# Value sums of two key blocks in one run on TensorE, every eighth step, in three attention layers

## The chip, the cores and the metric

The kernel runs on one core of one Trainium2 chip. The metric is device time in microseconds of one execution; lower is better. One core has TensorE (PE in the profile; its weight loads are PEld), VectorE (DVE), ScalarE (ACT), GpSimd (POOL) and SyncE (SP, which issues the DMAs here). Each has its own queue and runs it in order; the engines meet only at semaphores.

## The reference

Eight batches of 512 tokens, 256 wide, go through eight layers, each added to its input. Three of them are multi-head attention with 16 heads of 16, and only these are touched:

```python
x = x + _L0_attn_a_ref(_layernorm(x), ...)   # "decay": scores scaled by exp(-0.01*|t-s|)
x = x + _L0_ffn_ref(...)
x = x + _L0_attn_b_ref(_layernorm(x), ...)   # "rope"
x = x + _L0_ffn_ref(...)
x = x + _L1_attn_a_ref(...)                  # "causal", one head
x = x + _L1_ffn_ref(...)
x = x + _L1_attn_b_ref(_layernorm(x), ...)   # "latent": rotary, factored k and v
x = x + _L1_ffn_ref(...)

# inside each of the three, for b batches and 16 heads
scores = jnp.einsum('bhqd,bhkd->bhqk', q, k) * scale
attn = jax.nn.softmax(scores, axis=-1)
out = jnp.einsum('bhqk,bhkd->bhqd', attn, v)
out = out.transpose(0, 2, 1, 3).reshape(b, s, d) @ Wo
```

## The kernel before

`mha_layer` builds each of the three layers. A batch has four groups of four heads, and each group has four blocks of 128 keys. This makes 16 blocks of a batch, counted `kk` = 0 to 15, and 64 steps `s` = 0 to 63, one for each block and head. All engines run the same list of steps; what an engine does at a step is written out by hand in its own `body`.

At a step TensorE does, in this order:

- `exp_scores` (L1331, in decay L1334 and L1337): the transposed scores, keys by queries, of one head and key block, into one of two banks of `psB` ("scores_k"). It waits until ScalarE has taken the scores of two steps earlier.
- at some steps `value_sums` (L1362): four products, one for each head, of 32 columns of `Vaug` (values and ones) with the probabilities of one block, into four strips of one bank `psO` ("out_heads"). In fp32 each product is two instructions, so one call is a run of 8 matmuls.
- `max_scores` (L1318): the scores of a later group, queries by keys, for its row maxima, into a ring of banks of `psA` ("scores_q"): three banks in rope and latent, two in decay. It waits until VectorE has taken the maximum of the bank's last user.
- at the steps in `USES` one piece of `work`: projections for the next batch (L1281, L1286), transposes (L1277, L1292, L1297, L1300) and the output projection (L1305).

ScalarE takes each `exp_scores` into `probs` (L1489, "probs") and copies the work out. It starts a block only when `value_sums` of the block whose place in `probs` it takes is done; `probs` has `PSLOTS` places, three in decay and two in the others. VectorE takes a row maximum at each step (L1570, in decay L1567), splits the maxima of a group at one step in 16 (L1590 to L1597), normalises heads (L1604, L1606), adds the output (L1619 to L1627) and rotates keys and queries (L1553 to L1556); the rest of the rotation is on GpSimd.

In decay the diagonal of a block needs other scores: after every fourth `exp_scores` TensorE makes four products of 128 columns (L1347) into a bank of its own, ScalarE exponentiates them, and VectorE merges them into `probs` (`merge_diagonal`, L1579). The next four products (L1347) wait for that merge, since they write the same bank.

`value_sums` of block `kk` stands at step 4(`kk`+1) + `PV_AT`, and `PV_AT` is 2 in rope and latent, 3 in decay: at steps 2, 6, 10, ... 62, or 3, 7, 11, ... 63, where the one at step 2 or 3 belongs to the last block of the batch before. Four of them in a row make a group, after which ScalarE copies `psO` to `Osb` (L1480) and the heads' transposes may start.

Of the kernel before, what the change touches and what calls it, by code (L numbers as in the profile page):

```python
# [13 lines left out]
NB, S, D = 8, 512, 256  # L14
# [953 lines left out]
def mha_layer(nc, g, ins, decay, scale, project_q, biased, aside=(), results=None):  # L968
# [25 lines left out]
    if decay:  # L994
        PV_AT = 3
# [4 lines left out]
    elif project_q:  # L1000
        PV_AT = 2
# [4 lines left out]
    else:  # L1006
        PV_AT = 2
# [11 lines left out]
    A_BANK = [a % A_RING for a in range(63)] + [1]  # L1019
    A_LAST = [max(i for i in range(-64, a) if A_BANK[i % 64] == A_BANK[a]) for a in range(64)]  # L1020
    ROW_DMAS = NV
    PSLOTS = 3 if decay else 2
    XN = 4 if project_q else 8
    KQ = ["k0", "q0", "k1", "q1"] if project_q else ["k0", "k1"]
    PRO = ["xT0", "xT1"] + KQ + ["v0", "v1"]
    PREV = ["OT3", "aT0", "aT1", "Wo0", "Wo1"]
    assert USES == sorted(USES) and {n for _, n in USES} == {*PRO, *PREV, "OT0", "OT1", "OT2", "mT0", "mT1", "mT2", "mT3"}
    MID = [n for _, n in USES]
    ORDER = {"pre": PRO + ["mT0"], "first": [n for n in MID if n not in PREV], "mid": MID,
             "last": [n for n in MID if n not in PRO + ["mT0"]], "post": PREV}  # L1030
# [20 lines left out]
    def bank(tag, b, name):  # L1051

        return use(tag, 1 if tag == "mid" else b, name) % 2

    def emptied(tag, b, name):

        if tag != "mid":
            return use(tag, b, name) // 2 + 1
        return (b - 1) * (len(MID) // 2) + (use(tag, 1, name) // 2 + 1)

    def groups(s, tag, at):


        return [(g // 4, g % 4, a) for g in range(6) for a in range(len(at[g % 4])) if 16 * g + at[g % 4][a] == s
                and not (tag == "last" and g > 3)]

    with ExitStack() as ctx:
        def sb(name, shape, dt):
            return ctx.enter_context(nc.sbuf_tensor(f"{g['layer']}_{name}", shape, dt))
# [16 lines left out]
        KS = sb("KS", [99, NV, 2, 8, S], BF16)  # L1086
        probs = sb("probs", [P, PSLOTS, 4, S], F32)
        Vaug = sb("Vaug", [P, 2, 4, H, 32], F32)
# [171 lines left out]
        def _(pe):  # L1260
# [48 lines left out]
            def max_scores(nb, grp, a):  # L1309

                k = grp * NAG + a
                if a == 0:
                    pe.wait_ge(grp_loaded[grp], (nb + 1) * (16 * 2 * NV))
                if not (isinstance(nb, int) and nb * 64 + A_LAST[k] < 0):
                    pe.wait_ge(a_done, nb * 64 + (A_LAST[k] + 1))
                c, (qt, h) = grp // 2, divmod(a, 4)
                hh = 4 * (grp % 2) + h
                pe.matmul(psA[:, A_BANK[k], :], QS[0:96, 0, c, hh, qt * P:(qt + 1) * P],  # L1318
                          KS[0:96, NV - 1, c, hh, :], start=True, stop=True).then_inc(a_ready, 1)
# [31 lines left out]
            def value_sums(b, kk):  # L1351

                grp, kt = kk // 4, kk % 4
                if kk == 0:
                    for of in ("v0", "v1"):
                        at = ("pre", 0, of) if b == 0 else ("first" if b == 1 else "mid", b - 1, of)
                        pe.wait_ge(m_taken[bank(*at)], emptied(*at))
                if kt == 0 and not (isinstance(b, int) and b * 4 + grp < 1):
                    pe.wait_ge(o_taken, b * 4 + grp)
                pe.wait_ge(merged if decay else exp_done, (b * 16 + (kk + 1)) * (1 if decay else 4))  # L1360
                for h in range(4):
                    last = pe.matmul(psO[32 * h:32 * h + 32, :], Vaug[:, b % 2, kt, 4 * grp + h, :],  # L1362
                                     probs[:, (b * 16 + kk) % PSLOTS, h, :], start=(kt == 0), stop=(kt == 3))
                last.then_inc(pv_done, 1)
# [17 lines left out]
            def body(tag, b):  # L1382
                for s in range(64):
                    grp, o = divmod(s, 16)
                    exp_scores(b, s)
                    if o % 4 == PV_AT:
                        if s > PV_AT:
                            value_sums(b, s // 4 - 1)
                        elif tag != "first":
                            value_sums(b - 1, 15)  # L1390
                    for ahead, of, a in groups(s, tag, A_AT):
                        max_scores(b + ahead, of, a)
                    for at, name in USES:
                        if at == s and name in ORDER[tag]:
                            nb = b - 1 if name in PREV else b + 1 if name in PRO + ["mT0"] else b
                            work(tag, b, nb, name)

            body("first", 0)
            for b in range(1, NB - 1):
                body("mid", b)  # L1400
            body("last", NB - 1)
            value_sums(NB - 1, 15)
            for name in ORDER["post"]:
                work("post", NB, NB - 1, name)

# [2 lines left out]
        def _(act):  # L1408
# [73 lines left out]
            def body(tag, b):  # L1482
                for s in range(64):
                    grp, o = divmod(s, 16)
                    kk, h = s // 4, s % 4
                    if h == 0 and not (isinstance(b, int) and b * 16 + kk < PSLOTS):
                        act.wait_ge(pv_done, b * 16 + kk - PSLOTS + 1)
                    act.wait_ge(b_ready, b * 64 + (s + 1))
                    act.activation(probs[:, (b * 16 + kk) % PSLOTS, h, :], psB[:, s % 2, :], ACT.Exp, scale=scale).then_inc(  # L1489
                        exp_done, 1)  # L1490
# [27 lines left out]
        def _(dve):  # L1518
# [53 lines left out]
            def merge_diagonal(b, kk):  # L1572

                kt = kk % 4
                if b * 16 + kk == 0:
                    dve.wait_ge(later_set, 2)
                dve.wait_ge(exp_done, b * 64 + (4 * kk + 4))
                dve.wait_ge(e_exp, b * 16 + (kk + 1))
                dve.copy_predicated(probs[:, (b * 16 + kk) % PSLOTS, :, kt * P:(kt + 1) * P],  # L1579
                                    later[:, :].bitcast(mybir.dt.uint32).unsqueeze(1).to_broadcast([P, 4, P]),  # L1580
# [478 lines left out]
def hybrid_stack(nc, w, out):  # L2059

    with ExitStack() as ctx:
# [19 lines left out]
        with layer("decay"):  # L2081
            mha_layer(nc, g, decay, True, 1.0 / D ** 0.5, True, False, clears(g, w["zeros"]))
# [4 lines left out]
        with layer("experts1"):  # L2087
            routed_layer(nc, g, experts_a, False, then=lambda results: named(
                "rope", mha_layer, rope, False, HD ** -0.5, True, False, (), results))
        with layer("experts2"):  # L2090
            routed_layer(nc, g, experts_a, False, then=lambda results: named("causal", single_head_layer, causal, results))
        with layer("experts3"):
            routed_layer(nc, g, experts_b, True, then=lambda results: named(
                "latent", mha_layer, latent, False, HD ** -0.5, False, True, (), results))
# [75 lines left out]
```

## Time and profile before

| | |
|---|---|
| median of 3 runs | 3416.64 us (3415.6 to 3421.77) |
| the profiled execution | 3420.55 us, of which the span is 3418.5 us |
| PE busy | 2686.4 us (79%) |
| DVE busy | 1931.8 us (57%) |
| ACT busy | 1487.5 us (44%) |
| POOL busy | 780.6 us (23%) |
| out_heads matmuls | 1024 in each of decay, rope and latent, 137 to 148 us busy each |
| decay, first to last out_heads | 115.9 to 804.3 us |
| rope | 1091.4 to 1638.8 us |
| latent | 2486.0 to 3031.0 us |

The busy time of a matmul in these records is longer than the time it keeps the next one away, since matmuls are pipelined: the distance from one start to the next tells what a matmul costs TensorE. So a busy share near 100% does not mean that TensorE never waits. A row of a timeline gives the start, the duration, the engine, the line, what is written and read, how many alike were merged, and in brackets the idle time before it with what ended it.

### The profile page before, as it was taken

Reading aid. Unit: us, or ns where it says so; the run is one execution under the profiler, and the core shown is the slowest. Engines: PE = TensorE matmul, PEld = TensorE weight load, DVE = VectorE, ACT = ScalarE, POOL = GpSimd, SP = SyncE. Lnnn points to the kernel's source line nnn. Section 1 sums busy time; section 2 is a strip of 40 time slices with the busy share of each in tenths; the row PEclk is TensorE's granted clock in tenths of the full one; section 3 lists DMA queues with packets and bytes.
Section 4 is the critical chain, followed back from the end, with each engine's and each line's share of the span. In section 5 each row is a group of like instructions: output and inputs, shape, how many; then the busy total and the mean of one; then the engine's idle time right before and its main releaser. Section 6 shows DMA issues by size and latency. Waiting matters only on the chain. (4 is left out here: it accounts for less than half of the span.)

```text
span 3418.5 us, 40272 instructions
## 1 busy us (share of the span) xinstructions
PE 2686.4 (79%) x12980; PEld 1387.0 (41%) x12980; DVE 1931.8 (57%) x4955; ACT 1487.5 (44%) x2908; POOL 780.6 (23%) x742
## 2 busy tenths in 40 slices
PE   4868888896566999999555784898398999974993
PEld 2324443444342333333344564565133333343662
DVE  4757777785338778787342442111778788741112
ACT  2446666665223666666522431111166566640110
POOL 0312222210313322240123003000334323203003
PEclk6779999999687999999787895899599999986997
DMA  7555554441244322222134002232422332202333
GB/s 236 172 175 149 149 150 148 142 132 42 87 140 123 109 87 85 84 84 66 56 109 134 1 1 85 97 111 71 119 75 86 113 91 83 77 9 98 111 111 111
DMA packets 213575, 351.27 MB, mean 103 GB/s; under 512 B 21192, under 2 KB 168265, under 8 KB 208632
## 3 DMA queue, kind: packets, MB, share of 16 engines
q1 hardware_dynamic: 197864, 299.02, 28.0%
q0 software_dynamic: 15504, 49.68, 4.4%
q8 instruction: 107, 1.75, 0.2%
q14 instruction: 100, 0.82, 0.1%
HBM read 203.21 MB, written 154.80 MB: 105 GB/s over the span
## 5 line engine op out<-in xcount | busy, mean ns | idle before, releaser
L1567 DVE CUSTOM_DVE_ANT_0 decay_junk<-decay_scores_q,decay_corr 128x512 bf16<-128x512 f32 x512 | 338.9, 685 | 159.0 <-PE decay_scores_q L1318 157.5
L1489 ACT ACTIVATE decay_probs<-decay_scores_k 128x512 f32<-128x512 f32 x512 | 298.7, 602 | 229.3 <-PE decay_scores_k L1337 179.2
L1570 DVE TENSOR_REDUCE rope_mx<-rope_scores_q 128x1 f32<-128x512 f32 x512 | 326.5, 684 | 106.6 <-PE rope_scores_q L1318 106.6
L1489 ACT ACTIVATE latent_probs<-latent_scores_k 128x512 f32<-128x512 f32 x512 | 292.6, 600 | 207.4 <-PE latent_scores_k L1331 206.6
L1489 ACT ACTIVATE rope_probs<-rope_scores_k 128x512 f32<-128x512 f32 x512 | 293.0, 600 | 204.3 <-PE rope_scores_k L1331 203.5
L1570 DVE TENSOR_REDUCE latent_mx<-latent_scores_q 128x1 f32<-128x512 f32 x512 | 326.9, 684 | 96.8 <-PE latent_scores_q L1318 96.8
L1318 PE MATMUL latent_scores_q<-latent_KS,latent_QS 96*128 96x512 bf16 x512 | 204.1, 401 | 73.9 <-DVE latent_mx L1570 59.3
L1318 PE MATMUL decay_scores_q<-decay_KS,decay_QS 96*128 96x512 bf16 x512 | 213.8, 418 | 48.6 <-DVE decay_mx L1567 32.5
L1318 PE MATMUL rope_scores_q<-rope_KS,rope_QS 96*128 96x512 bf16 x512 | 202.7, 398 | 42.9 <-DVE rope_mx L1570 33.8
L1331 PE MATMUL latent_scores_k<-latent_QS,latent_KS 99*128 99x512 bf16 x512 | 197.0, 387 | 10.4 <-ACT latent_probs L1489 6.3
L1331 PE MATMUL rope_scores_k<-rope_QS,rope_KS 99*128 99x512 bf16 x512 | 196.5, 386 | 9.0 <-ACT rope_probs L1489 6.3
L1334 PE MATMUL decay_scores_k<-decay_QS,decay_KS 99*128 99x384 bf16 (+3 forms) x512 | 160.5, 315 | 54.1 <-ACT decay_probs L1489 26.9
L1318 PEld LDWEIGHTS latent_scores_q<-latent_KS,latent_QS 96*128 96x128 bf16 x512 | 50.1, 98 | 248.4 <-DVE latent_mx L1570 180.1
L1362 PE MATMUL decay_out_heads<-decay_probs,decay_Vaug 128*32 128x512 f32 x1024 | 147.8, 652 | 0.8 <-DVE decay_probs L1579 0.8
L1318 PEld LDWEIGHTS decay_scores_q<-decay_KS,decay_QS 96*128 96x128 bf16 x512 | 51.4, 101 | 228.4 <-DVE decay_mx L1567 164.1
L1362 PE MATMUL latent_out_heads<-latent_probs,latent_Vaug 128*32 128x512 f32 x1024 | 139.7, 618 | 0.7 <-ACT latent_probs L1489 0.7
L1362 PE MATMUL rope_out_heads<-rope_probs,rope_Vaug 128*32 128x512 f32 x1024 | 137.1, 608 | 0.7 <-ACT rope_probs L1489 0.7
L1318 PEld LDWEIGHTS rope_scores_q<-rope_KS,rope_QS 96*128 96x128 bf16 x512 | 50.2, 98 | 207.4 <-DVE rope_mx L1570 144.3
L1166 POOL CAST decay_parts<-decay_fc 128x512 bf16<-128x512 f32 x56 | 34.2, 611 | 410.9 <-DVE decay_fc L1553 398.9
L495 POOL DMA_INDIRECT experts_XN<-cap_results,experts_back x64 | 63.0, 984 | 262.5 <-DMA cap_results<-experts4x_y 243.5
L344 POOL DMA_INDIRECT cap_dispatched<-experts_XN,experts_slot x64 | 62.9, 983 | 250.3 <-SPq L58 200.2
L624 PE MATMUL experts4x_inner<-experts4x_xT,experts4x_w 128*128 128x512 f32 x256 | 113.4, 602 | 0.8 <-ACT experts4x_xT L662 0.8
(450 smaller groups left out, 5318.5 us busy)
## 6 DMA issues: line engine op xcount, KB each, us to landing
decay_parts_dram<-decay_parts SPq DMA_DIRECT2D x64, 384.0 KB, 2.6
decay_KS<-decay_parts_dram SPq DMA_DIRECT2D x64, 384.0 KB, 6.1
decay_QS<-decay_parts_dram SPq DMA_DIRECT2D x64, 384.0 KB, 6.6
decay_parts_dram<-decay_parts SPq DMA_DIRECT2D x64, 256.0 KB, 2.9
experts3x_w<-in_w_dram SPq DMA_DIRECT2D x16, 1024.0 KB
experts4x_w<-in_w_dram SPq DMA_DIRECT2D x16, 1024.0 KB
rope_parts_dram<-rope_parts SPq DMA_DIRECT2D x32, 384.0 KB, 2.9
rope_KS<-rope_parts_dram SPq DMA_DIRECT2D x32, 384.0 KB, 4.0
```

The lines of the kernel that those rows point to most:

```text
L344: pool.indirect_dma_start(out=xe, out_offset=bass.IndirectOffsetOnAxis(ap=g["slot"][:, i:i + 1], axis=0), in_=g["XN"][:, i, :], in_offset= ...
L495: pool.indirect_dma_start(out=g["XN"][:, i, :], out_offset=None, in_=ye, in_offset=bass.IndirectOffsetOnAxis(ap=g["back"][:, i:i + 1], axi ...
L624: last = pe.matmul(psH[:, f % 2, :], w1[:, p, c, f * P:(f + 1) * P], xT[:, p, c, :], start=(c == 0), stop=(c == 1))
L1166: eng.tensor_copy(parts[:, (nb * NCH + j) % RING, 0, :], fc[:, j % 2, :]).then_inc(p0_done, 1)
L1318: pe.matmul(psA[:, A_BANK[k], :], QS[0:96, 0, c, hh, qt * P:(qt + 1) * P], KS[0:96, NV - 1, c, hh, :], start=True, stop=True).then_inc(a_r ...
L1331: last = pe.matmul(psB[:, s % 2, :], KS[:, 0, c, hh, keys], QS[:, 0, c, hh, :], start=True, stop=True)
L1334: last = pe.matmul(psB[:, s % 2, 0:end], KS[:, 1, c, hh, keys], QS[:, 0, c, hh, 0:end], start=True, stop=True)
L1362: last = pe.matmul(psO[32 * h:32 * h + 32, :], Vaug[:, b % 2, kt, 4 * grp + h, :], probs[:, (b * 16 + kk) % PSLOTS, h, :], start=(kt == 0) ...
L1489: act.activation(probs[:, (b * 16 + kk) % PSLOTS, h, :], psB[:, s % 2, :], ACT.Exp, scale=scale).then_inc(exp_done, 1)
L1567: dve.tensor_tensor_reduce(junk[:, a % 2, :], psA[:, A_BANK[k], :], corr[:, qt, :], 1.0, -3.0e38, ALU.mult, ALU.max, mx[:, grp % 2, qt, h: ...
L1570: dve.tensor_reduce(mx[:, grp % 2, qt, h:h + 1], psA[:, A_BANK[k], :], AX.X, ALU.max).then_inc(a_done, 1)
```

## The change

In all three layers `probs` gets three places (`PSLOTS`), and the value sums of two blocks are made one after the other, at every eighth step: blocks 2m and 2m+1 at step 8(m+1) + `PV_AT`. In rope and latent the runs at steps 6, 14, 22, ... 62 go, and those at 2, 10, 18, ... 58 are twice as long; in decay those at 7, 15, ... 63 go, and those at 3, 11, ... 59 are twice as long. What is computed, every other instruction and every other place stay.

```diff
-    PSLOTS = 3 if decay else 2
+    PSLOTS, PV_BLOCKS = 3, 2
...
-                    if o % 4 == PV_AT:
-                        if s > PV_AT:
-                            value_sums(b, s // 4 - 1)
-                        elif tag != "first":
-                            value_sums(b - 1, 15)
+                    if s % (4 * PV_BLOCKS) == PV_AT:
+                        for kk in range(s // 4 - PV_BLOCKS, s // 4):
+                            if s > PV_AT:
+                                value_sums(b, kk)
+                            elif tag != "first":
+                                value_sums(b - 1, 16 + kk)
...
             body("last", NB - 1)
-            value_sums(NB - 1, 15)
+            for kk in range(16 - PV_BLOCKS, 16):
+                value_sums(NB - 1, kk)
```

TensorE in the rope layer, a batch in the middle, from step 38 to step 42, before ("x4" counts the products of one call; L1331 is `exp_scores`, L1318 `max_scores`):

```order
L1331 MATMUL rope_scores_k<-rope_QS,rope_KS 128x512
L1362 MATMUL rope_out_heads<-rope_probs,rope_Vaug 32x512 x4
L1318 MATMUL rope_scores_q<-rope_KS,rope_QS 128x512
L1331 MATMUL rope_scores_k<-rope_QS,rope_KS 128x512
L1318 MATMUL rope_scores_q<-rope_KS,rope_QS 128x512
L1331 MATMUL rope_scores_k<-rope_QS,rope_KS 128x512
L1318 MATMUL rope_scores_q<-rope_KS,rope_QS 128x512
L1292 MATMUL rope_work<-identb,rope_mp 12x128 x4
L1331 MATMUL rope_scores_k<-rope_QS,rope_KS 128x512
L1318 MATMUL rope_scores_q<-rope_KS,rope_QS 128x512
L1331 MATMUL rope_scores_k<-rope_QS,rope_KS 128x512
L1362 MATMUL rope_out_heads<-rope_probs,rope_Vaug 32x512 x4
```

And after, the same steps:

```order
L1331 MATMUL rope_scores_k<-rope_QS,rope_KS 128x512
L1318 MATMUL rope_scores_q<-rope_KS,rope_QS 128x512
L1331 MATMUL rope_scores_k<-rope_QS,rope_KS 128x512
L1318 MATMUL rope_scores_q<-rope_KS,rope_QS 128x512
L1331 MATMUL rope_scores_k<-rope_QS,rope_KS 128x512
L1318 MATMUL rope_scores_q<-rope_KS,rope_QS 128x512
L1292 MATMUL rope_work<-identb,rope_mp 12x128 x4
L1331 MATMUL rope_scores_k<-rope_QS,rope_KS 128x512
L1318 MATMUL rope_scores_q<-rope_KS,rope_QS 128x512
L1331 MATMUL rope_scores_k<-rope_QS,rope_KS 128x512
L1362 MATMUL rope_out_heads<-rope_probs,rope_Vaug 32x512 x8
```

The run at step 38 has moved behind everything up to step 42 and stands there with the run that was there already.

TensorE in the decay layer, from the run at step 43 to `max_scores` of step 47, before (L1347 is the products of the diagonal):

```order
L1362 MATMUL decay_out_heads<-decay_probs,decay_Vaug 32x512 x4
L1318 MATMUL decay_scores_q<-decay_KS,decay_QS 128x512
L1334 MATMUL decay_scores_k<-decay_QS,decay_KS 128x512
L1318 MATMUL decay_scores_q<-decay_KS,decay_QS 128x512
L1334 MATMUL decay_scores_k<-decay_QS,decay_KS 128x512
L1318 MATMUL decay_scores_q<-decay_KS,decay_QS 128x512
L1334 MATMUL decay_scores_k<-decay_QS,decay_KS 128x512
L1318 MATMUL decay_scores_q<-decay_KS,decay_QS 128x512
L1334 MATMUL decay_scores_k<-decay_QS,decay_KS 128x512
L1347 MATMUL decay_scores_q<-decay_QS,decay_KS 128x128 x4
L1362 MATMUL decay_out_heads<-decay_probs,decay_Vaug 32x512 x4
L1318 MATMUL decay_scores_q<-decay_KS,decay_QS 128x512
```

And after:

```order
L1362 MATMUL decay_out_heads<-decay_probs,decay_Vaug 32x512 x8
L1318 MATMUL decay_scores_q<-decay_KS,decay_QS 128x512
L1334 MATMUL decay_scores_k<-decay_QS,decay_KS 128x512
L1318 MATMUL decay_scores_q<-decay_KS,decay_QS 128x512
L1334 MATMUL decay_scores_k<-decay_QS,decay_KS 128x512
L1318 MATMUL decay_scores_q<-decay_KS,decay_QS 128x512
L1334 MATMUL decay_scores_k<-decay_QS,decay_KS 128x512
L1318 MATMUL decay_scores_q<-decay_KS,decay_QS 128x512
L1334 MATMUL decay_scores_k<-decay_QS,decay_KS 128x512
L1347 MATMUL decay_scores_q<-decay_QS,decay_KS 128x128 x4
L1318 MATMUL decay_scores_q<-decay_KS,decay_QS 128x512
```

The run at step 43 is twice as long, and none stands between the diagonal and `max_scores` of step 47.

## Rows read from the trace of the kernel before

**Rows 1.** The profile page: its first line.

```profile
span 3418.5 us, 40272 instructions
```

**Rows 2.** Stretch and length; busy PE, PEld, DVE, ACT, POOL; clock; DMA share, GB/s.

```profile
230.00:760.00 530.00, 471.66 (x2862) 213.62 (x2858) 411.42 (x1178) 345.24 (x653) 139.75 (x144) 0.95 0.49 145
1120.00:1610.00 490.00, 462.14 (x2431) 176.70 (x2430) 389.15 (x788) 317.85 (x597) 135.98 (x121) 1.00 0.29 88
```

**Rows 3.** Who waited for whom: total us, times, longest; TensorE.

```profile
PE rope_scores_q L1318 <- DVE rope_mx L1570: 33.8, 29, 7.8
PE decay_scores_q L1347 <- DVE decay_probs L1579: 19.4, 22, 2.1
```

**Rows 4.** The costliest groups of the page: one layer's value sums.

```profile
L1362 PE MATMUL rope_out_heads<-rope_probs,rope_Vaug 128*32 128x512 f32 x1024 | 137.1, 608 | 0.7 <-ACT rope_probs L1489 0.7
```

**Rows 5.** Timeline of rope, step 6 of a middle batch: TensorE and its weight loads.

```profile
1303.62 0.38 PE L1331 MATMUL rope_scores_k<-rope_QS,rope_KS 99*128 99x512 bf16 x1
1303.93 1.07 PE L1362 MATMUL rope_out_heads<-rope_probs,rope_Vaug 128*32 128x512 f32 x8
1304.92 0.39 PE L1318 MATMUL rope_scores_q<-rope_KS,rope_QS 96*128 96x512 bf16 x1
...
1303.92 0.16 PEld L1362 LDWEIGHTS rope_out_heads<-rope_probs,rope_Vaug 128*32 128x32 f32 x8 [0.64 <-issue]
```

**Rows 6.** Timeline of rope, steps 42 to 46: TensorE, then ScalarE.

```profile
1349.91 0.39 PE L1318 MATMUL rope_scores_q<-rope_KS,rope_QS 96*128 96x512 bf16 x1
1350.13 0.38 PE L1331 MATMUL rope_scores_k<-rope_QS,rope_KS 99*128 99x512 bf16 x1
...
1352.02 1.06 PE L1362 MATMUL rope_out_heads<-rope_probs,rope_Vaug 128*32 128x512 f32 x8
1353.02 0.39 PE L1318 MATMUL rope_scores_q<-rope_KS,rope_QS 96*128 96x512 bf16 x1
...
1350.55 2.17 ACT L1489 ACTIVATE rope_probs<-rope_scores_k 128x512 f32<-128x512 f32 x4 [0.43 <-PE rope_scores_k L1331]
```

**Rows 7.** Timeline of rope, steps 38 to 42: TensorE, then VectorE.

```profile
1347.52 0.39 PE L1318 MATMUL rope_scores_q<-rope_KS,rope_QS 96*128 96x512 bf16 x1 [0.70 <-DVE rope_mx L1570]
...
1346.78 1.28 DVE L1570 TENSOR_REDUCE rope_mx<-rope_scores_q 128x1 f32<-128x512 f32 x2
```

**Rows 8.** Timeline of decay, steps 45 to 48: VectorE, then TensorE.

```profile
459.62 0.72 DVE L1579 COPY_PREDICATED decay_probs<-decay_later,decay_scores_q 128x512 f32<-128x512 uint32 x1
460.24 0.67 DVE L1567 CUSTOM_DVE_ANT_0 decay_junk<-decay_scores_q,decay_corr 128x512 bf16<-128x512 f32 x1
...
462.16 0.69 DVE L1567 CUSTOM_DVE_ANT_0 decay_junk<-decay_scores_q,decay_corr 128x512 bf16<-128x512 f32 x1 [0.62 <-PE decay_scores_q L1318]
...
457.97 0.39 PE L1318 MATMUL decay_scores_q<-decay_KS,decay_QS 96*128 96x512 bf16 x1
...
460.40 0.40 PE L1347 MATMUL decay_scores_q<-decay_QS,decay_KS 99*128 99x128 bf16 x4
460.73 1.07 PE L1362 MATMUL decay_out_heads<-decay_probs,decay_Vaug 128*32 128x512 f32 x8
461.73 0.39 PE L1318 MATMUL decay_scores_q<-decay_KS,decay_QS 96*128 96x512 bf16 x1
```

**Rows 9.** Timeline of decay, steps 15 to 19, TensorE; then a stretch's clock.

```profile
414.18 1.06 PE L1362 MATMUL decay_out_heads<-decay_probs,decay_Vaug 128*32 128x512 f32 x8
...
418.66 0.29 PE L1334 MATMUL decay_scores_k<-decay_QS,decay_KS 99*128 99x128 bf16 x1 [2.65 <-ACT decay_probs L1489]
...
421.97 1.94 PE L1362 MATMUL decay_out_heads<-decay_probs,decay_Vaug 128*32 128x512 f32 x8
...
417.80:421.20 3.40, 2.08 (x8) 0.80 (x9) 1.31 (x3) 3.40 (x8) 2.90 (x4) 0.50 0.28 94
```

**Rows 10.** Timeline of rope, step 24, TensorE; then a stretch of latent, step 26.

```profile
1326.86 0.39 PE L1318 MATMUL rope_scores_q<-rope_KS,rope_QS 96*128 96x512 bf16 x1 [1.54 <-DVE rope_mx L1570]
...
2718.40:2721.80 3.40, 3.40 (x13) 0.81 (x12) 2.07 (x4) 2.06 (x4) 2.61 (x3) 0.50 0.31 103
```

## The prediction

> **What bounds the kernel now.** I read the busy shares by stretch, then the waits, then timelines of a batch in the middle. The profiled execution took 3420.55 us, 3418.5 of them span [rows 1] and 2 around it; the median of the runs, 3416.64, is 3.91 us lower, and I add what the trace gives to the median as it is. In the steady part of rope TensorE is busy 462 of 490 us, VectorE 389 and ScalarE 318; in decay 472, 411 and 345 of 530 [rows 2]. TensorE leads, but the busy time of pipelined matmuls flatters it, and the waits show that it isn't alone: in rope it stands 33.8 us behind VectorE's maxima, in decay 19.4 us behind the merge of the diagonal alone [rows 3]. So for each stretch of a batch one has to ask which engine ends last in it. A step below is one of a batch's 64.
>
> **What joining saves.** A layer has 1024 out_heads matmuls in runs of 8 [rows 4], so 128 runs; 64 of them move to stand behind another, 192 in the three layers. A score matmul keeps the next one away for 0.22 us (1349.91 to 1350.13 [rows 6]), but the run for 0.31: 1303.62 to 1303.93. So the way in costs 0.09. The next matmul starts at 1304.92, 0.99 later; I use 1.00 [rows 5]. One of the eight takes 0.61 [rows 4] and the whole run 1.07 [rows 5], so the second wave of four starts 0.45 after the first. Two waves are 0.90, and 0.10 is the way out. Both ends are late weight loads: the run's starts at 1303.92, with its matmul and not ahead of it [rows 5]. A run of 16 is then 1.00 + 2 x 0.45 = 1.90, and a pair costs 0.09 + 1.90 = 1.99 in place of 2 x 1.09 = 2.18: **0.19 us less**. No row shows a run of 16 without a wait inside. The bounds are 0 (the second call pays both ends again) and 0.19 (nothing but the ends can go); I take 0.19, as the strips stay the same. In all 192 x 0.19 = 36 us: the ceiling.
>
> The Trainium skill, "TensorE: Matmul & The Clock Gate", section "Step-by-step: what each phase is for", says that a weight load is pulled ahead of running matmuls if its rows don't conflict or it goes to the background buffer. If that held here, the ends would not be late loads and joining would save nothing. The late load of [rows 5] speaks against it where the shape of the tiles changes.
>
> **What the third place saves.** Nothing that I can find: the wait of ScalarE in [rows 6] is for scores, not for out_heads. With the joined run a block still finds its place free: block 2m+3 starts after the run that holds block 2m. So it adds no wait either. SyncE's, GpSimd's and VectorE's instructions keep their order; no DMA is moved past another.
>
> **What bunching costs.** TensorE now gives no scores for 0.31 + 1.90 = 2.2 us and then runs eight steps without a pause. ScalarE has two banks of scores ahead of it, VectorE three (two in decay). They run dry in the long run and hold TensorE up between runs. Where TensorE is the bound, a removed run is 1.09 less and a doubled one 0.90 more. Where it isn't, the first may give nothing.
>
> *Rope and latent, steps 43 to 50: ScalarE.* Four steps take 1353.02 - 1349.91 = 3.11 us; four exponentials take 2.17 and one about 0.60, so they follow each other at (2.17 - 0.60) / 3 = 0.52 [rows 6]. With no run between, four more steps go at 0.52 each, 2.09, where TensorE alone would need 4 x 0.44 = 1.76. A pair: 3.11 + 2.09 + 0.90 = 6.10, in place of 6.22: **0.1 less**.
>
> *The same, steps 36 to 42: VectorE.* Step 40's `max_scores` waits 0.70 for VectorE, which works without a gap up to the two maxima at 1346.78 [rows 7]. The run of step 38 lies under that work. Taken away it frees nothing, as the same maximum releases step 40; the doubled run at 42 stands in the open. **0.9 more.**
>
> *Steps 14 to 26.* VectorE's long stretch begins with `max_scores` of step 14, which comes 1.09 sooner. The runs at 18 and 22 lie under it: step 24 waits 1.54 [rows 10]. The run of 26 is open, 0.90 longer: 0.2 less. Step 10: 0.2 less in rope, and 0.3 in latent, where VectorE is still busy and lets only part of the 1.09 through. Steps 34, 58 and 2: about 0. A batch: rope -0.1 + 0.9 - 0.2 - 0.2 = **+0.4**, latent **+0.3**.
>
> *Decay, steps 43 to 59: the merge.* VectorE merges at 459.62 and is done at 460.24; the diagonal goes at 460.40, the run at 460.73, the next `max_scores` at 461.73, and VectorE takes it up at 462.16 after 0.62 idle. Four steps are 461.73 - 457.97 = 3.76, and outside the 0.62 VectorE never rests [rows 8]: 1.24 in two loops. After: from merge to maximum 1.92 + 0.90 = 2.82, of which two waiting maxima cover 1.92 - 0.62 = 1.30, so 1.52 idle, and none at the other diagonal. **0.3 more** a pair; at 51 nothing covers it.
>
> *Decay, steps 11 to 27.* At step 16 TensorE stands 2.65 us behind ScalarE [rows 9]. By the code ScalarE waits there for VectorE's fourth rotation, which stands behind the maximum of step 15, which stands behind the run at 414.18; that run goes, so 1.09 sooner. But right behind this idle time the granted clock is 0.50, the 1.2 GHz level, and step 19's run lies there: 1.94 us in place of 1.07 [rows 9]. Doubled it is 1.8 more. From there VectorE bounds it to step 26, so the removal at 23 gives nothing, and the doubling at 27 costs 0.90. Sum -1.1 + 1.8 + 0.9 = **+1.6**. Bounds: -0.4 (two pairs that keep their 0.19) and +2.7 (nothing comes sooner at 16).
>
> *The rest of decay.* Step 3: +0.2, 11: -0.2, 35: +0.1, 59: 0, by the same working. Step 43: -0.3, between -0.9 and +0.9, since the removed run of 39 lies partly open at the low clock. A batch of decay: 0.3 + 1.6 - 0.2 = **+1.7**.
>
> **The sum.** I count seven batches of a layer like the middle ones: 7 x (1.7 + 0.4 + 0.3) = 16.8. The last batch has hardly any maxima, so four steps are about 3.11 - 0.22 = 2.89; a pair goes from 5.78 to 2.89 + 2.09 + 0.90 = 5.88, 0.1 x 8 pairs x 3 layers = 2.4. Together 19 us: **3436 us**. I prefer this to the ceiling because behind most removed runs that I followed another engine's wait comes within a few steps.
>
> **Rivals.** *Faster: TensorE is the bound after all.* The place is the removed runs of steps 22, 38 and their like. If the banks were deep enough that VectorE gets through sooner when scores come sooner, each pair would keep its 0.19: 36 us, 3380; with half the pairs 18 us, 3399. It decides as soon as the waits behind removed runs grow by less than 0.9 us. For it: a busy share of 94% in rope [rows 2]. Against: [rows 3] and [rows 7].
>
> *No change: the costs are half of mine.* With -0.4 in place of +1.6 in decay the sum is 19 - 14 = 5 us, and with half the price at step 42 (14 batches x 0.45 = 6) it is 0: 3410 to 3423. For it: that term has the widest bounds.
>
> *Slower still: the clock.* TensorE's wait at step 24 in rope grows from 1.54 us to some 2.6, as the run of 22 goes and the maximum comes no sooner relative to it [rows 10]. Decay's clock was down behind 2.65 us of standing [rows 9], latent's is in step 26 already, rope's isn't. A stretch of 3.40 us fully busy at 0.50 [rows 10] loses 1.7: in seven batches of rope 12 us, as much again in latent if it comes twice: 3447 to 3460. The skill's section "Loop structure matters more than you think" on that page warns of waits between matmuls in the same sense; the 0.50 of [rows 9] agrees.
>
> **How the numbers follow.** Forecast (3424 to 3447) 0.44; TensorE bound 0.20; no change 0.22; clock 0.14. The range 3396 to 3460 leaves out the better half of the first rival and the tail of the last. 0.2% of 3416.64, 6.8 us, is about what a measurement can tell from no change; it holds the no-change case. Faster 0.20, same 0.22, slower 0.58.
>
> **What would show it.** A run of 16: 1.90 from its start to the next matmul, and 0.31 ahead of it. Rope: the wait of step 40 near 1.8, that of step 24 over 2; steps 43 to 50 in 6.1 us, decay's in 7.8. Decay: step 19's run lasts near 3.7. I am wrong if TensorE's waits behind L1567 and L1570 don't grow, or if rope's batches get shorter.

## The result and the profile after

The median of the changed kernel is 3479.91 us (5 runs, 3478.73 to 3485.95) beside 3415.6 us (5 runs, 3414.2 to 3421.77) of the kernel before: 64 us more, a ratio of 1.0191 with a 95% interval of 1.0177 to 1.0205. The direction was forecast; the size was not: 19 us more were forecast, and the range ended at 3460. Lines of the kernel from L1403 on stand two lines later than before.

The page's first lines, beside [rows 1]:

```profile
span 3484.0 us, 40270 instructions
...
PE 2733.9 (78%) x12980; PEld 1420.7 (41%) x12980; DVE 1926.4 (55%) x4955; ACT 1483.4 (43%) x2908; POOL 784.6 (23%) x742
```

The stretch of decay of [rows 2] and one of rope like the one there, 3 us longer, then the three layers from the start of their first exponential to that of their last (stretch and length; busy PE, PEld, DVE, ACT, POOL; granted clock; DMA share, GB/s):

```profile
230.00:760.00 530.00, 466.36 (x2735) 216.12 (x2735) 389.27 (x1131) 329.57 (x624) 139.68 (x143) 0.92 0.48 143
1132.00:1625.00 493.00, 458.75 (x2327) 181.83 (x2325) 373.52 (x753) 301.19 (x568) 139.41 (x125) 0.95 0.30 89
...
104.40:821.30 716.90, 611.51 (x3592) 280.81 (x3590) 500.81 (x1449) 435.72 (x825) 169.81 (x172) 0.91 0.46 140
1100.40:1676.90 576.50, 533.39 (x2700) 209.17 (x2698) 427.73 (x865) 355.76 (x670) 157.75 (x140) 0.96 0.26 78
2515.30:3090.70 575.40, 518.91 (x2644) 192.29 (x2642) 434.14 (x889) 350.39 (x656) 173.78 (x146) 0.96 0.26 78
```

The three layers before:

```profile
105.00:801.20 696.20, 596.77 (x3592) 267.71 (x3590) 508.52 (x1449) 437.26 (x825) 168.12 (x172) 0.92 0.47 144
1083.00:1638.70 555.70, 519.35 (x2707) 197.28 (x2709) 425.95 (x862) 358.23 (x671) 157.28 (x140) 0.99 0.27 81
2478.00:3029.70 551.70, 505.58 (x2652) 188.05 (x2650) 432.88 (x888) 351.88 (x657) 171.39 (x146) 0.98 0.27 81
```

They grew by 20.7, 20.8 and 23.7, together 65.2 of the 65.5 us by which the span grew. So all of it lies in the layers that were changed, and 42 us of it in TensorE's busy time (1621.7 to 1663.8), though nothing was added for it to do. The clock of rope's steady part is 0.95 where it was 1.00 [rows 2].

TensorE's waits, beside [rows 3]:

```profile
PE latent_scores_q L1318 <- DVE latent_mx L1572: 61.7, 44, 23.4
PE rope_scores_q L1318 <- DVE rope_mx L1572: 37.7, 27, 7.9
PE decay_scores_q L1318 <- DVE decay_mx L1569: 36.5, 81, 10.6
...
PE decay_scores_q L1347 <- DVE decay_probs L1581: 19.0, 24, 2.1
```

The maxima are waited for 2 to 4 us longer in each layer (33.8 us before in rope, 59.3 in latent, 32.5 in decay), the merge as long as before (19.4). Waits alone don't hold 65 us. The timelines show the rest. Rope, steps 24 to 26 of a middle batch, TensorE; the second fence has the clock of the stretches around it:

```profile
1348.48 0.39 PE L1331 MATMUL rope_scores_k<-rope_QS,rope_KS 99*128 99x512 bf16 x1
1351.29 0.61 PE L1318 MATMUL rope_scores_q<-rope_KS,rope_QS 96*128 96x512 bf16 x1 [2.42 <-DVE rope_mx L1572]
...
1353.74 3.64 PE L1362 MATMUL rope_out_heads<-rope_probs,rope_Vaug 128*32 128x512 f32 x16
1357.31 0.61 PE L1318 MATMUL rope_scores_q<-rope_KS,rope_QS 96*128 96x512 bf16 x1
```

```profile
1347.60:1351.00 3.40, 1.24 (x5) 0.29 (x3) 3.30 (x6) 1.85 (x4) 3.26 (x4) 1.00 0.00 0
1351.30:1354.70 3.40, 3.40 (x16) 0.98 (x20) 2.91 (x6) 1.71 (x4) 2.21 (x3) 0.50 0.09 32
1354.70:1358.10 3.40, 3.40 (x18) 0.94 (x11) 0.14 (x1) 0.35 (x1) 1.10 (x1) 0.51 0.61 203
```

TensorE is busy 1.24 of 3.40 us while it waits for VectorE, and behind that the granted clock is 0.50, the 1.2 GHz level, for almost 7 us. The doubled run lies there: 3.57 us from 1353.74 to 1357.31. The trace of before has the same place at full clock in five of its six middle batches, with a run of 1.00 us.

The same batch, steps 38 to 43, where the clock was full:

```profile
1374.57 0.39 PE L1318 MATMUL rope_scores_q<-rope_KS,rope_QS 96*128 96x512 bf16 x1 [0.93 <-DVE rope_mx L1572]
...
1375.89 0.39 PE L1318 MATMUL rope_scores_q<-rope_KS,rope_QS 96*128 96x512 bf16 x1 [0.70 <-DVE rope_mx L1572]
...
1376.97 0.38 PE L1331 MATMUL rope_scores_k<-rope_QS,rope_KS 99*128 99x512 bf16 x1
1377.28 1.92 PE L1362 MATMUL rope_out_heads<-rope_probs,rope_Vaug 128*32 128x512 f32 x16
1379.14 0.39 PE L1318 MATMUL rope_scores_q<-rope_KS,rope_QS 96*128 96x512 bf16 x1
```

This gives the price of a run of 16: 0.31 ahead of it and 1.86 to the next matmul; at the 1.2 GHz level it is 3.58. It also shows where the removed run went: a wait of 0.93 at step 39, with the 0.70 of step 40 as in [rows 7].

Decay, step 16, the run of step 19, the wait of step 24's maximum, and the run of step 27:

```profile
424.58 0.23 PE L1334 MATMUL decay_scores_k<-decay_QS,decay_KS 99*128 99x128 bf16 x1 [2.65 <-ACT decay_probs L1491]
...
427.81 2.80 PE L1362 MATMUL decay_out_heads<-decay_probs,decay_Vaug 128*32 128x512 f32 x16
430.54 0.39 PE L1318 MATMUL decay_scores_q<-decay_KS,decay_QS 96*128 96x512 bf16 x1
...
435.77 0.39 PE L1318 MATMUL decay_scores_q<-decay_KS,decay_QS 96*128 96x512 bf16 x1 [0.90 <-DVE decay_mx L1569]
...
441.24 1.92 PE L1362 MATMUL decay_out_heads<-decay_probs,decay_Vaug 128*32 128x512 f32 x16
```

The 2.65 us of [rows 9] are unchanged. The doubled run took 2.73 us here, two thirds of that time at the low clock, and 3.3 to 3.6 in the five other middle batches.

### The profile page after: what moved, and what is told of

The parts are those of the page before. It is cut to its first block and busy times, and to the rows that moved or that the text cites. A ratio compares the mean times of both kernels' runs of the same rounds, so it can differ in the third digit from the quotient of the medians.

```text
span 3484.0 us, 40270 instructions
## 1 busy us (share of the span) xinstructions
PE 2733.9 (78%) x12980; PEld 1420.7 (41%) x12980; DVE 1926.4 (55%) x4955; ACT 1483.4 (43%) x2908; POOL 784.6 (23%) x742
## 5 line engine op out<-in xcount | busy, mean ns | idle before, releaser
L1318 PE MATMUL latent_scores_q<-latent_KS,latent_QS 96*128 96x512 bf16 x512 | 203.5, 399 | 78.6 <-DVE latent_mx L1572 61.7
L1318 PE MATMUL decay_scores_q<-decay_KS,decay_QS 96*128 96x512 bf16 x512 | 212.7, 416 | 52.2 <-DVE decay_mx L1569 36.5
L1318 PE MATMUL rope_scores_q<-rope_KS,rope_QS 96*128 96x512 bf16 x512 | 205.6, 403 | 46.9 <-DVE rope_mx L1572 37.7
L1331 PE MATMUL latent_scores_k<-latent_QS,latent_KS 99*128 99x512 bf16 x512 | 200.2, 392 | 16.8 <-ACT latent_probs L1491 12.3
L1331 PE MATMUL rope_scores_k<-rope_QS,rope_KS 99*128 99x512 bf16 x512 | 200.0, 392 | 12.2 <-ACT rope_probs L1491 7.7
L1334 PE MATMUL decay_scores_k<-decay_QS,decay_KS 99*128 99x384 bf16 (+3 forms) x512 | 161.4, 316 | 55.5 <-ACT decay_probs L1491 30.3
L1318 PEld LDWEIGHTS latent_scores_q<-latent_KS,latent_QS 96*128 96x128 bf16 x512 | 50.2, 98 | 201.1 <-DVE latent_mx L1572 115.9
L1318 PEld LDWEIGHTS decay_scores_q<-decay_KS,decay_QS 96*128 96x128 bf16 x512 | 50.9, 100 | 191.5 <-DVE decay_mx L1569 112.1
L1318 PEld LDWEIGHTS rope_scores_q<-rope_KS,rope_QS 96*128 96x128 bf16 x512 | 50.5, 99 | 163.1 <-DVE rope_mx L1572 91.8
```

Source lines behind the costliest of these rows:

```text
L1331: last = pe.matmul(psB[:, s % 2, :], KS[:, 0, c, hh, keys], QS[:, 0, c, hh, :], start=True, stop=True)
L1334: last = pe.matmul(psB[:, s % 2, 0:end], KS[:, 1, c, hh, keys], QS[:, 0, c, hh, 0:end], start=True, stop=True)
```

## The experiments

All ran on two other chips (e1 to e4 on one, e5 to e10 on the other), where the kernel before took 3333 us. The attention layers are as long there as here (696, 556 and 553 us with only the places changed), so the layers of all traces may be compared; ratios are against the kernel before on the same chip. A ratio rests on 4 to 10 executions of a kernel, its trace on one of them. Most traces are within about 6 us of their kernel's median, but that of e2 is 9 us below the median, the fastest of ten, and that of e6 15 us above it, the slowest of nine. Two edits were used. JOINED names the pairs whose two runs are joined (the pair 8 moves the run of step 6 to step 10 in rope and latent, and that of 7 to 11 in decay; 16, 24 and 40 likewise); all eight are the change itself. FILL repeats a step's `exp_scores` matmul (in decay the product of L1334) so many times in batches 1 to 6, called the middle batches here, with the same operands and the same bank, so that TensorE works where it waited. Shortened:

```diff
+    FILL = {'decay': {16: 38, ...}, 'rope': {24: 10, ...}, 'latent': {...}}[...]
+    JOINED = {'decay': [...], 'rope': [...], 'latent': [...]}[...]
...
+                for i in range(FILL.get(s, 0) if fill else 0):
+                    last = pe.matmul(psB[:, s % 2, :], KS[:, 0, c, hh, keys], QS[:, 0, c, hh, :], start=True, stop=True) \
+                        if not decay else ...
```

What the traces give, in us. "Low" is the time at the 1.2 GHz level in the three layers, from each one's second batch on.

| kernel | ratio, 95% interval | decay | rope | latent | sum | low |
|---|---|---|---|---|---|---|
| before (first chip) | | 696.2 | 555.7 | 551.7 | 1803.6 | 72 |
| after (first chip) | 1.0191 [1.0177, 1.0205] | 716.9 | 576.5 | 575.4 | 1868.8 | 171 |
| e1_places | 1.0005 [0.9987, 1.0023] | 695.7 | 555.5 | 552.8 | 1803.9 | 79 |
| e2_after_fill | 1.0021 [1.0007, 1.0035] | 685.6 | 559.6 | 554.2 | 1799.3 | 10 |
| e3_before_fill | 0.9977 [0.996, 0.9995] | 689.2 | 554.8 | 545.7 | 1789.7 | 17 |
| e4_single42 | 1.0127 [1.0098, 1.0157] | 715.9 | 565.6 | 560.7 | 1842.2 | 140 |
| e5_cross | 1.0115 [1.0085, 1.0144] | 714.5 | 563.5 | 564.0 | 1842.0 | 109 |
| e6_two | 0.995 [0.9933, 0.9966] | 705.9 | 552.1 | 540.3 | 1798.4 | 123 |
| e7_two_fill | 0.989 [0.9862, 0.9918] | 675.5 | 550.8 | 541.5 | 1767.8 | 20 |
| e8_other_two | 1.0192 [1.0161, 1.0224] | 707.0 | 578.1 | 573.9 | 1859.0 | 136 |
| e9_rope24 | 0.9874 [0.9852, 0.9896] | 671.9 | 544.9 | 541.7 | 1758.5 | 3 |
| e10_24filled | 1.0044 [1.0022, 1.0066] | 697.1 | 561.0 | 551.7 | 1809.8 | 24 |

And by place, mean of batches 1 to 5, us from the first exponential of a stretch of steps to the first behind it:

| steps | before | after | e3 | e2 | e9 | e10 |
|---|---|---|---|---|---|---|
| decay 5-12 | 11.78 | 11.40 | 11.78 | 11.40 | 11.40 | 11.78 |
| decay 13-28 | 25.89 | 28.00 | 26.22 | 25.20 | 23.71 | 27.43 |
| decay 37-44 | 11.10 | 12.29 | 10.08 | 10.23 | 10.08 | 10.08 |
| decay 45-60 | 16.69 | 16.98 | 16.71 | 17.00 | 16.71 | 16.70 |
| rope 5-20 | 19.54 | 19.16 | 19.54 | 19.16 | 19.16 | 19.54 |
| rope 21-28 | 12.54 | 14.79 | 12.22 | 12.35 | 11.58 | 13.16 |
| rope 37-44 | 7.41 | 8.93 | 7.41 | 8.27 | 7.41 | 7.41 |
| rope 45-60 | 13.12 | 13.20 | 13.12 | 13.20 | 13.12 | 13.13 |
| latent 5-20 | 18.23 | 18.22 | 18.24 | 18.22 | 18.23 | 18.24 |
| latent 21-28 | 12.68 | 13.59 | 11.72 | 12.02 | 11.18 | 12.57 |
| latent 37-44 | 7.41 | 9.92 | 7.41 | 8.27 | 7.42 | 7.42 |
| latent 53-68 | 16.45 | 16.72 | 16.50 | 16.72 | 16.51 | 16.51 |

**Places alone.**

```diff
-    PSLOTS = 3 if decay else 2
+    PSLOTS = 3
```

> The kernel before with three places for probabilities in all layers and every value sum where it was. Both theories: no difference, ratio within 0.1% of 1, since no wait for a place was seen. If the third place alone costs (another address, another wait), it shows here: then part of the 64 us is not the order of TensorE.

The ratio is 1.0005, with 1 inside its interval, and the layers' sum 0.3 us off: no cost and no gain of the third place can be seen, and everything else below is the joined runs and the filling.

**The change with its idle time filled** (decay 16, 24 and 39; rope 24, 39 and 40; latent 11, 24, 39 and 40).

> The changed kernel, but in batches 1 to 6 some score matmuls are issued again, with the same operands to the same bank, before their semaphore: in decay 38 more at step 16, 4 at 24 and 15 at 39, in rope 10 at 24, 4 at 39, 3 at 40, in latent 5 at 11, 9 at 24, 4 at 39, 3 at 40. They are as long as TensorE stands idle there in the trace after, a little less, and add nothing to the result. Theory clock (the three layers spend 171 us at half clock in the trace after, 72 in that before, and a stretch busy with matmuls loses half of it): half-clock stretches of the three layers fall from 171 us to under 70 and the time by 35 to 60 us, near 3435, where my sum without the clock rival had it. Theory banks alone (only waits and doubled runs that stand open cost, the clock nothing): no gain, 0 to 10 us slower through the added matmuls.

In the traces 69.5 us are gone, more than the change's 65 (1868.8 to 1799.3); by the ratios (1.0191 to 1.0021) it is 57. The only difference is more work for TensorE in its waits. Rope, step 24 to 26, TensorE (L1342 is the repeated matmul, L1320 `max_scores`, L1368 the value sums):

```profile
1279.22 2.32 PE L1342 MATMUL rope_scores_k<-rope_QS,rope_KS 99*128 99x512 bf16 x10
1281.80 0.39 PE L1320 MATMUL rope_scores_q<-rope_KS,rope_QS 96*128 96x512 bf16 x1 [0.26 <-DVE rope_mx L1580]
...
1283.19 1.92 PE L1368 MATMUL rope_out_heads<-rope_probs,rope_Vaug 128*32 128x512 f32 x16
1285.05 0.39 PE L1320 MATMUL rope_scores_q<-rope_KS,rope_QS 96*128 96x512 bf16 x1
```

The maximum of step 24 is waited for until the same point of the batch, but the run behind it takes 1.86 in place of 3.57.

**The kernel before, filled likewise** (decay 16 and 39, rope 24, latent 11 and 24; three places).

> The kernel before with three places and with matmuls issued again in the same way: in decay 38 at step 16 and 15 at 39, in rope 6 at 24, in latent 6 at 11 and 6 at 24, batches 1 to 6. Theory clock: before has 72 us at half clock in the three layers, 48 of them in those batches of decay behind steps 16 and 39; most go, 15 to 30 us faster than before. Theory banks alone: same or up to 5 us slower.

The kernel before gives back 14 us in its layers and 8 by the ratio, less than the 15 to 30 I expected. Set against e2, 55 of the 65 us are the clock by the traces and 10 (1799.3 - 1789.7) the moved runs; by the ratios 49 and 15. Most of the loss is the clock either way; its share is known no closer than that.

In decay the comparison is blurred, for something else came in with the filling: steps 13 to 20 became 1.4 us shorter (14.17 to 12.76), but steps 21 to 28 1.7 longer (11.72 to 13.46). There, in batch 1 of e3 and at full clock, VectorE splits the maxima (two of its four instructions), then GpSimd, then TensorE's wait for the merge that stands behind the split:

```profile
247.25 1.00 DVE L1595 TENSOR_SCALAR decay_mp<-decay_mx 128x16 bf16<-128x16 f32 x1
248.29 1.18 DVE L1597 SCALAR_TENSOR_TENSOR decay_mr<-decay_mx,decay_mp 128x16 f32<-128x16 f32 x1
...
247.06 1.16 POOL L1169 TENSOR_TENSOR decay_rr<-decay_fc,decay_parts 128x512 f32<-128x512 f32 x1
248.28 1.15 POOL L1174 TENSOR_TENSOR decay_parts<-decay_rr,decay_parts 128x512 bf16<-128x512 f32 x1
...
250.57 0.40 PE L1352 MATMUL decay_scores_q<-decay_QS,decay_KS 99*128 99x128 bf16 x4 [2.14 <-DVE decay_probs L1584]
```

In the kernel before each of the four takes 0.17 here. Now two take 1.00 and 1.18, and each ends 0.03 to 0.04 us after the GpSimd instruction beside it. This came in four of e3's six middle batches, and all ten such instructions of its decay layer that took over 0.3 us ran beside one of GpSimd's. Below I call this the slow split. The earlier arrival put them there and lost what it had won; that GpSimd is what holds them is my reading, which no run tests. Rope and latent have two such slow instructions a batch at this place in every kernel (1.25 and 1.13 in rope), so they don't disturb the comparison there.

**One pair single again** (rope and latent without pair 40; all else as the change).

> The changed kernel, but in rope and latent the runs at steps 38 and 42 stay single, as before; all else joined. Theory banks with clock: the open doubled run at 42 goes, 0.86 us in each of 14 batches, 12 us, and with it the half-clock stretches at steps 41 and 42 (2 in rope, 6 in latent, 1.6 us each), 13 us: together 20 to 28 us faster than the changed kernel, and batches of rope near 73.9, of latent near 72.5. Theory clock alone: 13. Theory that every joined pair costs alike (64 us over 192 pairs): 16 pairs make 5 us.

Rope and latent lose 10.9 and 14.7 us of what they had gained in length, 25.6 in 14 batches. e2 and e3 put the open run at 8.27 - 7.41 = 0.86 a batch at full clock, 12 us; the rest is mostly the clock at that place, 0.66 a batch in rope and 1.65 in latent (after against e2). Rope also lost 0.7 a batch in steps 21 to 28 (14.79 to 14.10), which weren't edited.

**The filling crossed** (rope only at 24; latent only at 39 and 40; decay not).

> The changed kernel with matmuls issued again at one place a layer only: in rope 10 at step 24, in latent 4 at 39 and 3 at 40, in decay none; batches 1 to 6. Theory that a half-clock stretch belongs to the idle time just ahead of it: in rope the stretches at steps 24 to 26 go (34 us of half clock in the changed kernel) and those at 41 and 42 stay or become more, in latent those at 42 go (20 us) and those at 24 to 26 stay; decay as in the changed kernel, 717 us long. Rope 560 to 568 us long in place of 577, latent 565 to 568 in place of 576: 17 to 25 us faster than the changed kernel. Theory that it is the mean load of the batch that counts: both places change alike in both layers.

Latent of this kernel, steps 24 to 26, then steps 40 to 42, TensorE:

```profile
2673.11 0.59 PE L1320 MATMUL latent_scores_q<-latent_KS,latent_QS 96*128 96x512 bf16 x1 [2.15 <-DVE latent_mx L1580]
...
2675.55 2.40 PE L1368 MATMUL latent_out_heads<-latent_probs,latent_Vaug 128*32 128x512 f32 x16
...
2677.89 0.39 PE L1320 MATMUL latent_scores_q<-latent_KS,latent_QS 96*128 96x512 bf16 x1
```

```profile
2697.51 1.92 PE L1368 MATMUL latent_out_heads<-latent_probs,latent_Vaug 128*32 128x512 f32 x16
2699.36 0.39 PE L1320 MATMUL latent_scores_q<-latent_KS,latent_QS 96*128 96x512 bf16 x1
```

Where the idle time stood, the run behind it is slow in five of six middle batches (2.34 us here, up to 3.58); where it was filled, 1.86 in every batch. In rope it is the other way round: the run of step 26 takes 1.86 in all middle batches and that of 42 still takes 3.2 to 3.4 in two. Rope is 563.5 and latent 564.0 us long, close to what the first theory had (560 to 568 and 565 to 568). The low clock belongs to the idle time right ahead of it, and not to how hard TensorE works in the layer.

**Only the pairs 8 and 16.**

> Only two pairs of a batch are joined, those whose run goes from steps 6 and 14 to steps 10 and 18 (decay 7 and 15 to 11 and 19); all others single, three places. My theory: a run gains where it is moved from ahead of VectorE's long stretch to under it. Per batch rope -0.24 and -1.1, latent -0.3 and -0.3 to -1.0, decay -0.4 and -1.1 (less 0.8 to 0.9 back where step 19's run is at half clock): rope 547 us long in place of 556, latent 546 to 549 in place of 552, decay 687 to 694 in place of 696. Together 12 to 25 us faster than the kernel before, ratio 0.993 to 0.996. Rival, joining always costs in proportion (64 us over 192 pairs): 48 pairs, 16 us slower. Rival, every join saves its 0.24: 12 us faster, the same in each layer, 4 us.

Faster than the kernel before: 0.995, as expected. The layers of the trace differ from what I expected: latent is shorter (540.3), rope longer (552.1, with 17 us at the low clock behind step 24), and decay 10 us longer than before, with 65 us at the low clock in steps 32 to 47 where the kernel before has 17. Decay, step 39, TensorE:

```profile
449.64 0.61 PE L1348 MATMUL decay_scores_q<-decay_QS,decay_KS 99*128 99x128 bf16 x4 [2.07 <-DVE decay_probs L1584]
450.18 1.94 PE L1363 MATMUL decay_out_heads<-decay_probs,decay_Vaug 128*32 128x512 f32 x8
452.05 0.61 PE L1319 MATMUL decay_scores_q<-decay_KS,decay_QS 96*128 96x512 bf16 x1
```

Nothing is edited there. The kernel before waits the same 2.1 us, and in two of its six middle batches the clock stays full around it; here it is down in all six. But this trace is of the slowest of nine executions. Its mean clock over the whole kernel is 0.886, the median of the nine 0.895, and 0.009 of 3320 us is 60 us more at the low level than in a typical execution (twice the missing share). So decay's low clock here may be that of one bad execution, and it isn't shown that joining elsewhere brings the clock down at this place. What the trace does show is that a wait of about 2 us may or may not bring the clock down. By what that is decided is open.

**The same, filled** (decay 16 and 39, latent 11 and 24).

> The kernel of e6_two and matmuls issued again in batches 1 to 6: in decay 44 at step 16 and 15 at 39, in latent 5 at 11 and 2 at 24. Clock theory: decay loses most of its half-clock stretches (55 us before) and 10 us more against e6_two, near 680; latent 2 to 5 us. Together 25 to 35 us faster than the kernel before, ratio 0.990 to 0.993. Without a part for the clock: as e6_two.

0.989, a little better than expected. Against e3, where decay and latent are filled at the same places and no run is joined, the layers are 22 us shorter (in e7 rope's step 24 isn't filled, which takes some of it back). Not all of that is the two pairs' own: 14 of the 22 are in decay, where e3 has the slow split and 17 us of low clock and e7 has 7.

**Only the pairs 24 and 40.**

> Only the pairs are joined whose run goes from steps 22 and 38 to steps 26 and 42 (decay 23 and 39 to 27 and 43): as many as in e6_two, 48 in all. My theory: both go from under VectorE's stretch into the open, 0.86 each, 1.7 us a batch and layer, 36 us, and 10 to 25 us for the clock, which falls as steps 24 and 39 idle longer: 35 to 60 us slower than the kernel before, ratio 1.011 to 1.018. Rival, cost in proportion: 16 us slower, as e6_two. Rival, each join saves: 12 us faster.

1.0192 (1.0161 to 1.0224): two of the eight pairs make as much as all eight. I expected 1.011 to 1.018.

**e7 and rope filled at 24**, the last place that had a low clock.

> Runs joined only at the pairs of steps 8 and 16, as in the kernel with two joined pairs and filled idle time; added are six repeats of the score matmul in the idle time of step 24 in rope, whose output is written again with the same numbers. Theory (what is left of the half clock in rope, 14 us of it behind step 24, comes from that idle time): rope goes from 550.8 us to 545 to 549, its half clock to under 3 us, the ratio from 0.989 to 0.987 to 0.9885. Rival (the fill only fills, and the half clock there is chance, or the repeats get in the way of the maximum of step 24): rope stays at 550 or more, the ratio at 0.989 or above.

Rope went from 550.8 to 544.9 and its low time to 0; 3 us are left, in decay. This is the fastest kernel here, 0.9874, 1.3% below the kernel before.

**Only the pair 24, filled.**

> Only the pair of step 24 is joined in all three layers (the runs of 22 or 23 go, those of 26 or 27 are doubled), three places, and the idle times of steps 11, 16, 24 and 39 are filled with repeats of the score matmul that write the same numbers. It shows what is left of the cost of the doubled run at step 26 and 27 when the clock stays up. Theory (the run stands in the open there for at most 0.9 us a pair, and the rest of what the kernel with two other pairs lost in steps 21 to 28, 1.7 us a batch in rope and 2.0 in latent, was the clock): steps 21 to 28 take 12.1 to 12.5 us in rope, under 12.3 in latent and 12.5 to 12.7 in decay, the half clock is under 20 us in the three layers, and the ratio is 0.998 to 1.001. Rival (the doubled run itself costs most of it, by holding up ScalarE and VectorE): rope stays above 13 us, latent above 14 in these steps, ratio above 1.005.

```profile
1306.60 1.92 PE L1368 MATMUL rope_out_heads<-rope_probs,rope_Vaug 128*32 128x512 f32 x16
1308.45 0.39 PE L1320 MATMUL rope_scores_q<-rope_KS,rope_QS 96*128 96x512 bf16 x1
```

Neither theory holds in full. The clock is up, and yet steps 21 to 28 take 13.16 in rope, 0.94 more than in e3, and 12.57 in latent, 0.85 more: the doubled run is paid in full, more than I allowed for. I had taken e2's 12.35 for that price and forgotten that e2 also has the pair 16, which gives 12.22 - 11.58 = 0.64 back in the same steps. In decay steps 13 to 28 take 1.2 more; it has 24 us of low clock that filling did not keep away, and the slow split of e3 in four batches.

## Why the prediction was right in direction and wrong in size

**The joined run.** Forecast 1.90, measured 1.86; 0.31 ahead of it held (0.15 behind L1347 in decay). A pair then saves 2.18 - 0.09 - 1.86 = 0.23, and the bound of 0.19 was too low: four products more take (1.86 - 1.00) / 2 = 0.43, not the 0.45 that I had read off two busy times. So 192 pairs are worth 44 us. Joining does save the ends of a run. The Trainium skill, "TensorE: Matmul & The Clock Gate", "Step-by-step: what each phase is for", has weight loads pulled ahead of running matmuls where the row groups don't conflict or the load goes to the background buffer. By that there would be no ends to save, and the 1.86 against twice 1.00 speaks against it here.

**The third place.** Right, as far as the interval tells: 1.0005 (0.9987 to 1.0023).

**Rope and latent, steps 43 to 50.** Forecast 0.1 less a pair (6.10), measured 0.04 more (6.22 to 6.27 in rope and 6.26 in latent). I had the exponentials follow each other at 0.52 us, from four of them. In e2 the eight between two runs take 4.47, (4.47 - 0.60) / 7 = 0.55 each, which is most of the miss.

**Steps 36 to 42.** Forecast +0.9, measured +0.86 at full clock. The mechanism was right. The sign to watch was off by a step: the wait did not grow at step 40, a new one came at step 39.

**Steps 14 to 26.** The wait of step 24 grew from 1.54 to 2.42 (forecast 2.6). At full clock the whole came to -0.14 in steps 13 to 20 and +0.13 in 21 to 28 of rope, and to +0.3 and +0.3 in latent, where I had written -0.2 for the whole in either layer. e9 and e10 take it apart: in rope pair 16 gives 0.78 and pair 24 costs 0.94, in latent 0.22 and 0.85. Why latent gains so little is open. Step 10 came as forecast (-0.24, -0.33).

**Decay, 43 to 59.** Forecast 0.3 a pair, where the cover is gone, measured 0.15 in each of steps 45 to 52 and 53 to 60. The chain is there: diagonal, run of 16, maximum, VectorE idle for 1.48 of the forecast 1.52:

```profile
473.39 0.40 PE L1347 MATMUL decay_scores_q<-decay_QS,decay_KS 99*128 99x128 bf16 x4
473.72 1.92 PE L1362 MATMUL decay_out_heads<-decay_probs,decay_Vaug 128*32 128x512 f32 x16
475.58 0.39 PE L1318 MATMUL decay_scores_q<-decay_KS,decay_QS 96*128 96x512 bf16 x1
...
476.00 0.69 DVE L1569 CUSTOM_DVE_ANT_0 decay_junk<-decay_scores_q,decay_corr 128x512 bf16<-128x512 f32 x1 [1.48 <-PE decay_scores_q L1318]
```

**Decay, 11 to 27.** Forecast +1.6, measured +2.1 in steps 13 to 28. Doubling at the low clock was seen: 3.3 to 3.6 us in five of six batches, against a forecast of 3.7. Not seen was that this too comes with a second low stretch at step 26.

**The step that failed** is the clock. I had the mechanism among the rivals and in the right words, with the wait of step 24 and the row of [rows 10], and gave it 0.14 and 12 to 24 us. Three things were wrong. It was kept out of the sum but for decay's step 19, though the sum itself forecast the longer wait. It was priced at one place of a batch, while the waits of step 39 and 40, which the same text forecast, brought it at step 42 too, and decay has it at 26 and 43. And it was priced at 1.7 us each time. Filling shows, in the traces, per batch (after less e2) 2.4 in rope and 1.6 in latent at steps 21 to 28, 0.7 and 1.7 at steps 37 to 44, and in decay 2.8 at 13 to 28 and 2.1 at 37 to 44: 11.2 us, in six batches 67 of the 69.5 that the layers became shorter (57 by the ratios), against the 12 to 24 of the rival. In the kernel before it was 2.0, less what the slow split took back. The doubled runs stand right behind the waits that joining makes longer, in the slow stretch, and in the open: such a run costs 1.72 more there, a single one 0.87.

The rest of the sum came out near, in part by luck. It held 13 us without the clock's 0.9 at decay's step 19 (19 less 7 x 0.9); e2 and e3 differ by 10 in their layers and by 15 in their medians. But a batch of rope became 0.7 longer where I had 0.4, one of latent 1.4 where I had 0.3, and one of decay 0.8 shorter where I had 0.8 longer, so the misses cancel. Decay's is e3's slow split: in four of six batches there, in one of e2. Put together from those batches of each stretch of steps that have neither it nor the low clock, a batch of decay takes 84.6 us in e2 and 83.8 in e3, 0.8 more, as forecast; no whole batch of e3 is like that. The rival "TensorE is the bound after all" holds for one kind of pair. Pairs 8 and 16 gain 31 us (e3 against e9). 17 of these are in decay, where e3 has the slow split and 17 us of low clock against 3; the 14 of rope and latent are 0.43 a pair. That is more than joining saves. I put it down to where the removed run stood, open ahead of VectorE's long stretch, while the doubled one lies beneath it; e6 was forecast by this, but no run tests it alone.

## What to carry to other kernels

Moving work on one engine pays by where it leaves and where it lands, not by what joining saves: 0.43 us a pair gained into cover (rope and latent), 0.9 lost a pair into the open, when the joining itself is worth 0.23. When an edit makes TensorE wait longer anywhere, ask which work stands right behind that wait and price it at the 1.2 GHz level too, at every such place, in the sum. And try work that nobody needs in TensorE's waits: repeated matmuls alone made the kernel before 0.23% faster (0.05 to 0.4) and the changed one 1.7% (1.0191 to 1.0021, on different chips). Look afterwards at what arrives sooner, as decay's split in e3. And before reading the clock out of one trace, compare that execution with the others of its kernel: e6's was 15 us off.

## What the runs showed of the hardware

TensorE's clock fell to the 1.2 GHz level behind waits of only 2 to 2.7 us, or behind two of 0.93 and 0.70 close together (steps 39 and 40 of the changed kernel, in all six middle batches of latent and two of rope), in layers where it is busy 85 to 93% of the time. It isn't settled by the length of the wait: in rope these two are alike in all six batches, and around the 2.1 us of decay's step 39 the clock was down in four of six middle batches before and in six of six after. The Trainium skill, "TensorE: Matmul & The Clock Gate", section "A second HAM failure mode: psum-queue depth-cycling", tells of a kernel whose short pauses between groups of matmuls make the clock go up and down; the trace agrees, with rope's clock at 0.95 after and 1.00 before, when the waits for maxima went from 33.8 to 37.7 us. Matmuls with old operands held the clock up in most batches: 171 us at the low level became 10 in the changed kernel and 72 became 17 in the one before. They cost nothing measurable where they fit into a wait: rope's steps 21 to 28 take 12.21 us unfilled and at full clock (five of e1's middle batches) and 12.22 filled (e3). Small VectorE instructions (128x16) took 1.0 to 1.3 us in place of 0.17, each time beside a GpSimd instruction (all 38 over 0.3 us in e3), though 34 others beside one stayed short.
